# Linear attention rewritten from four batches of eight heads to a pipeline of eight units of four heads

## The reference, cut to what matters

```python
H, DK, DV = (8, 128, 32)
GATE_NORM = 16.0
q = (x @ Wq).reshape(B, T, H, DK) * DK ** -0.5     # x is the layer norm of the input
k = (x @ Wk).reshape(B, T, H, DK)
v = (x @ Wv).reshape(B, T, H, DV)
gk = log_sigmoid(x @ Wgk0 @ Wgk1 + bgk1) / GATE_NORM
# per head: S_t = S_{t-1} * exp(gk_t)[:, None] + k_t^T v_t ;  o_t = q_t @ S_t
g = (x @ Wg).reshape(B, T, H, DV)
o = o * rsqrt(mean(o * o, axis=-1) + EPS)
o = o * g_norm_w * (g * sigmoid(g))
return o.reshape(B, T, H * DV) @ Wo
```

## Time and profile before

| | us |
|---|---|
| median of 3 runs | 1894.39 (1889.34 to 1896.7) |
| the profiled execution, its own time | 1890.36 |
| its span, first to last instruction | 1888.6 |
| linear attention in it, from the first row addition to the last addition to x | 319.77 to 728.97 |
| mean granted TensorE clock | 0.914 of 2.4 GHz |

### The profile page before, as it was taken

The page is one execution under the profiler, slowest core; times in us unless marked ns, Lnnn a source line. Parts: engine busy times, 40 slices in busy tenths (PEclk is TensorE's granted clock), DMA queues, the critical chain, the costliest instruction groups (busy, mean ns, idle before and its releaser), DMA issues. The chain is left out here.

```text
span 1888.6 us, 27025 instructions
## 1 busy us (share of the span) xinstructions
PE 1568.3 (83%) x7662; PEld 1041.7 (55%) x7662; DVE 1092.2 (58%) x2687; ACT 774.5 (41%) x1866; POOL 719.5 (38%) x831
## 2 busy tenths in 40 slices
PE   6869994866868687878996588789999999998798
PEld 4545663534444445545664466555666666665676
DVE  6832222475757546862222788656766766664688
ACT  5523332527171714533333111146655655553211
POOL 3534444440503001544443666035545545543000
PEclk9979997789898988888998788889999999999899
DMA  7209996110101003207995222000000000000000
GB/s 214 65 19 261 304 299 192 56 56 12 57 11 34 1 1 107 78 1 207 290 300 157 81 78 77 7 1 1 1 1 1 1 1 1 1 1 1 8 17 20
DMA packets 83387, 142.46 MB, mean 75 GB/s; under 512 B 15816, under 2 KB 43312, under 8 KB 83296
## 3 DMA queue, kind: packets, MB, share of 16 engines
q1 hardware_dynamic: 53600, 90.96, 16.4%
q0 software_dynamic: 15360, 37.77, 6.8%
q10 hardware_dynamic: 14336, 12.59, 2.3%
HBM read 122.39 MB, written 18.87 MB: 75 GB/s over the span
## 5 line engine op out<-in xcount | busy, mean ns | idle before, releaser
L2206 POOL TENSOR_TENSOR sb_m_prob<-sb_m_prob,sb_m_rinv 128x512 f32<-128x512 f32 x256 | 258.5, 1040 | 289.2 <-DVE sb_m_rinv L2255 289.2
L2162 ACT ACTIVATE sb_m_prob<-m_ps_s,sb_m_nmax 128x512 f32<-128x512 f32 x256 | 173.6, 683 | 204.4 <-DVE sb_m_nmax L2259 204.3
L2259 DVE TENSOR_REDUCE sb_m_nmax<-m_ps_s 128x2 f32<-128x1024 f32 x128 | 156.4, 1222 | 127.9 <-PE m_ps_s L2057 127.8
L1239 POOL DMA_INDIRECT sb_c_rows<-slot_rows,sb_c_at x192 | 193.5, 1008 | 74.7 <-issue 48.4
L1218 DVE TENSOR_TENSOR sb_e_h<-sb_e_sg,e_ps_gu 96x176 f32<-96x176 f32 x128 | 42.7, 334 | 261.7 <-ACT sb_e_sg L1194 261.7
L1156 PE MATMUL e_ps_gu<-e_wgu,sb_e_xT 128*96 128x352 f32 x512 | 178.4, 471 | 12.1 <-ACT sb_e_xT L1188 11.7
L1131 POOL DMA_INDIRECT sb_e_x<-xn_rows,sb_e_index x128 | 121.3, 948 | 102.9 <-POOL sb_e_index L104 96.4
L2065 PE MATMUL m_ps_p<-sb_ident,sb_m_prob 128*128 128x128 f32 x1024 | 136.4, 274 | 15.8 <-ACT sb_m_pT L2170 11.3
L2065 PEld LDWEIGHTS m_ps_p<-sb_ident,sb_m_prob 128*128 128x128 f32 x1024 | 117.9, 141 | 41.1 <-POOL sb_m_prob L2206 13.8
L1173 PE MATMUL e_ps_y<-e_wdn,sb_e_hT 96*96 96x256 f32 x512 | 132.3, 382 | 0.0
L2056 PE MATMUL m_ps_s<-sb_m_latT_high,sb_m_qa 128*128 128x512 f32 x256 | 126.7, 495 | 1.1 <-ACT sb_m_prob L2162 1.1
(11 more groups left out here) (274 smaller groups left out, 3298.1 us busy)
## 6 DMA issues: line engine op xcount, KB each, us to landing
e_wgu<-wgu SPq DMA_DIRECT2D x128, 352.0 KB, 4.7
e_wdn<-wdn SPq DMA_DIRECT2D x128, 192.0 KB, 4.3
slot_rows<-sb_e_y ACTq DMA_DIRECT2D x128, 96.0 KB, 4.2
xn_rows<-sb_r_xn SPq DMA_DIRECT2D x16, 256.0 KB, 2.2
sb_c_rows<-slot_rows,sb_c_at POOLq DMA_INDIRECT x192, 2.8
sb_x<-x SPq DMA_DIRECT2D x4, 512.0 KB, 5.5
sb_e_x<-xn_rows,sb_e_index POOLq DMA_INDIRECT x128, 4.7
sb_g_zm<-wqT SPq DMA_DIRECT2D x1, 2048.0 KB, 8.9
```

Of the source, the lines that this page charges most:

```text
L1239: pool.indirect_dma_start(rows[u][j][:, :], None, k.slot_rows[:, :], bass.IndirectOffsetOnAxis(ap=at[u][:, j:j + 1], axis=0))\
L2162: act.activation(prob[s % 4][:, hh, :], ps_s[s % 2][:, hh, :], ACT.Exp, bias=nmax[s % 2][:, hh:hh + 1], accum_out=rsum[s % 2][:, hh:hh + 1 ...
L2206: pool.tensor_tensor(part, part, rinv[s % 2][:, hh:hh + 1].to_broadcast([P, T]), ALU.mult)\
L2259: dve.tensor_reduce(nmax[s % 2][:, :], ps_s[s % 2][:, :, :], AX, ALU.max, negate=True).then_inc(nmax_ready, 1)
```

## The change

The work is cut into eight units of four heads: unit u is the lower or upper half of the heads of batch u // 2. One function `slot(u)` in each engine's list works on three units: the gates of unit u + 2, the projections, values and output gates of unit u + 1, and the recurrence of unit u. Slots run from -2 to 7. In slots -1, 1 and 3 the next batch is loaded (`loaded_batch`: layer norm, transposes, low-rank product); in slots 2, 4 and 6 a finished batch is projected and added to x (`output_batch`).

The gates are summed without the minimum: ScalarE writes the ReLU of -z in place of z, the running sum adds both inputs in one instruction and runs over all four chunks without a reset, and `edges` takes differences of the sums at middles and ends of chunks (five tiny instructions). One small exponential takes the place of three. The two long exponentials and the subtractions of the middle keep their sizes. The squares, the mean, the normalisation and the output gate are done once for a unit with 512 columns, straight from PSUM, in place of once for a chunk with 256. `xT`, `low`, `mv`, `gw` and the output's PSUM bank have two buffers each; `ps_out` is gone, and the output projection uses the ring. The row additions stand at other places of VectorE's list (tiles 4 to 7 in slot -2, then two tiles in each of slots -1 to 2), and GpSimd issues two tiles' gathers in each of its rounds.

The core of the diff (the bodies of the projections, copies and multiplies change only in their indices):

```diff
+            def gate_parts(u):
+                for h in range(HG):
+                    hh = u % 2 * HG + h
+                    src = use(act, "z", u, h)
+                    act.activation(za[:, u % 2, h, :], src[:, :], ACT.Abs, bias=k.bgk1[:, hh:hh + 1]).then_inc(abs_ready, 1)
+                    act.activation(zm[:, u % 2, h, :], src[:, :], ACT.Relu, scale=-1.0, bias=minus_b[:, hh:hh + 1])\
+                       .then_inc(freed("z", u, h), 1)
...
-                s.after(s.mark(dve.scalar_tensor_tensor(out=zm[:, hs, :], in0=zm[:, hs, :], scalar=0.0, in1=za[:, hs, :],
-                                                        op0=ALU.min, op1=ALU.subtract)))
-                for h in range(half * HG, (half + 1) * HG):
-                    n = s.mark(dve.tensor_tensor_scan(zm[:, h, :], k.chunk_keep[:, :], zm[:, h, :], 0.0, ALU.mult, ALU.add))
...
+            def gate_sums(u, heads):
...
+                    dve.tensor_tensor_scan(part, part, za[:, u % 2, h, :], 0.0, ALU.add, ALU.add).then_inc(sum_ready, 1)
...
+            def edges(u):
...
+                s.mark(dve.tensor_copy(mid[:, :, :], sums[:, :, :, MID]))
+                s.after(s.mark(dve.tensor_copy(ends[:, :, 1:], sums[:, :, :, SUB - 1])))
+                dve.tensor_tensor(spans[:, 0, :, :], mid[:, :, :], ends[:, :, 0:NSUB], ALU.subtract)
+                dve.tensor_tensor(spans[:, 1, :, :], ends[:, :, 1:], ends[:, :, 0:NSUB], ALU.subtract)
+                dve.tensor_tensor(spans[:, 2, :, :], ends[:, :, 1:], mid[:, :, :], ALU.subtract).then_inc(edge_ready, 1)
+                for h in range(HG):
+                    ins = dve.tensor_tensor(za[:, u % 2, h, :].rearrange("p (c s) -> p c s", s=SUB),
+                                            zm[:, u % 2, h, :].rearrange("p (c s) -> p c s", s=SUB),
                                             over(mid[:, h, :], SUB), ALU.subtract)
                 ins.then_inc(cen_ready, 1)
```

TensorE's slot, in which `r` holds for slots 0 to 7 and calls for units outside 0 to 7 do nothing:

```diff
+            def slot(u):
+                r, b_in, b_out = 0 <= u < U, loaded_batch(u), output_batch(u)
+                if r: scores(u, 0)
+                gate(u + 2, 0); projected(u + 1, 0)
+                gate(u + 2, 1); projected(u + 1, 1)
+                gate(u + 2, 2); gate(u + 2, 3)
+                if u >= 1: mean_squares(u - 1)
+                if r: keys_turned(u, 0)
+                projected(u + 1, 2)
+                if r: tiled(u, 0); turned_back(u, 0); scores(u, 1); keys_turned(u, 1)
+                projected(u + 1, 3); values(u + 1)
+                if r: tiled(u, 1)
+                projected(u + 1, 4)
+                if r: turned_back(u, 1)
+                output(b_out, 0); output(b_out, 1)
+                if r: scores(u, 2); keys_turned(u, 2)
+                output_gates(u + 1); projected(u + 1, 5)
+                if r: tiled(u, 2)
+                if b_in is not None: transposes(b_in)
+                projected(u + 1, 6)
+                if r: turned_back(u, 2)
+                output(b_out, 2); output(b_out, 3)
+                if r: scores(u, 3)
+                projected(u + 1, 7)
+                if r: tiled(u, 3)
+                if b_in is not None: low_rank(b_in)
```

ScalarE's and VectorE's slots (here with several calls on a line, as above):

```diff
+            def slot(u):     # ScalarE; zs: u + 2 < U, qs: 0 <= u + 1 < U
+                if b_in is not None: deviations(b_in)
+                if zs: gate_parts(u + 2)
+                if u >= 1: inverse_rms(u - 1)
+                if r: kT_copy(u, 0); kvT_copy(u, 0)
+                if zs: exps(u + 2)
+                if r: kT_copy(u, 1)
+                if zs: lns(u + 2)
+                if qs: value_copy(u + 1)
+                if r: kvT_copy(u, 1); kT_copy(u, 2)
+                if qs: gate_copies(u + 1)
+                if r: kvT_copy(u, 2)
+                if b_in is not None: xT_copies(b_in)
+                if qs: sigmoids(u + 1)
+                if zs: decays(u + 2)
+                if b_in is not None: low_copy(b_in)
+                if r: squares(u)
...
+            def slot(u):     # VectorE
+                n = 2 * u + 10
+                if u == -2: add_rows(4, range(TOPK)); statistics(4); add_rows(5, range(TOPK)); statistics(5)
+                if r: masked(u, 0)
+                scale(u + 1, 0); scale(u + 1, 1); scale(u + 1, 2)
+                if b_in is not None: normalise(b_in)
+                if r: kept = state_added(u, 0, kept)
+                add_rows(n, range(4))
+                if r: masked(u, 1); kept = state_used(u, 1, kept)
+                gate_sums(u + 2, range(1)); scale(u + 1, 3)
+                if u >= 1: normed(u - 1)
+                gate_sums(u + 2, range(1, 2)); scale(u + 1, 4)
+                if r: kept = state_added(u, 1, kept)
+                add_rows(n, range(4, 6)); statistics(n)
+                if r: masked(u, 2); kept = state_used(u, 2, kept)
+                add_out(b_out, 0); add_out(b_out, 1)
+                gate_sums(u + 2, range(2, 3)); scale(u + 1, 5); gate_sums(u + 2, range(3, 4))
+                edges(u + 2); scale(u + 1, 6)
+                if r: kept = state_added(u, 2, kept)
+                add_rows(n + 1, range(3))
+                add_out(b_out, 2); add_out(b_out, 3)
+                if r: masked(u, 3); kept = state_used(u, 3, kept)
+                scale(u + 1, 7)
+                add_rows(n + 1, range(3, 6)); statistics(n + 1)
+                if b_in is not None: low_parts(b_in)
```

More of the change, by code:

```diff
@@ L1288, in linear_attention @@
     a_free = [k.sem(f"g_bank_free{a}") for a in range(A)]
[L1290 to L1311, removed]
+    use_of = {}
     with ExitStack() as ctx:
@@ L1405, in low_rank @@
                     emptied(pe, "tr", b, j)
-                to = take("low", b, 0)
+                to = take("low", b)
                 for c in range(DC):
[L1408 to L1414, removed]
-                for h in heads:
-                    to = take("z", b, h)
-                    given(pe.matmul(to[:, :], wgk1[:, h * DK:(h + 1) * DK], low[:, :], start=True, stop=True), "z", b, h)
@@ L1419, in values @@
[L1419 to L1431 removed]
+                    ins = pe.matmul(to[:, :], k.wgk0[:, c, :], xT[b % 2][:, c, :], start=(c == 0), stop=(c == DC - 1))
@@ new lines, in low_rank, with gate, values @@
+                given(ins, "low", b)
+            def gate(u, h):
+                if u >= U:
+                    return
+                hh = u % 2 * HG + h
+                pe.wait_ge(low_split, batch_of(u) + 1)
+                to = take("z", u, h)
+                given(pe.matmul(to[:, :], wgk1[:, hh * DK:(hh + 1) * DK], low[batch_of(u) % 2][:, :], start=True, stop=True),
+                      "z", u, h)
+            def values(u):
+                if u >= U:
+                    return
+                to, x = take("v", u), xT[batch_of(u) % 2]
+                for j in range(TB):
@@ new lines, in projected @@
+            def projected(u, i):
+                if not 0 <= u < U:
+                    return
+                name, weights = ("q", k.wq0) if i < HG else ("k", k.wk0)
+                hh = u % 2 * HG + i % HG
+                to, x = take("qk", u, i), xT[batch_of(u) % 2]
+                for c in range(DC):
+                    ins = pe.matmul(to[:, :], weights[:, c, hh * DK:(hh + 1) * DK], x[:, c, :],
+                                    start=(c == 0), stop=(c == DC - 1))
+                given(ins, "qk", u, i)
@@ L1595, in z_copies @@
[L1595 to L1604 removed]
+                src = use(act, "low", b)
@@ L1757, in _, with gather @@
+            def gather(n):
+                if n < NT:
+                    gather_tile(pool, k, 0, n, n % 2, rows, at)
             pool.sem_inc(k.sem("c_rows_used"), 2)
@@ new lines, in state_added @@
+            def state_added(u, j, kept):
+                dve.wait_ge(edge_ready, 2 * u + 2)
+                dve.wait_ge(kv_ready, u * (TB - 1) + j + 1)
+                to = kv_dec if j else state
+                dve.tensor_tensor(to[:, :, :], ps_kv[:, :, :], over(edge[u % 3][:, 2, :, j], DV),
+                                  ALU.mult).then_inc(kv_used, 1)
+                dve.wait_ge(kv_used, u * (TB - 1) + j + 1)
+                if j:
+                    s.after(kept)
+                    return s.mark(dve.tensor_tensor(state[:, :, :], state[:, :, :], kv_dec[:, :, :], ALU.add))
+                return s.n
```

799 lines of the change are left out of this document (396 added, 403 removed).

## The result

The changed kernel takes 1845.18 us (median of 4 runs, 1841.6 to 1849.4); the kernel before took 1895.55 beside it (4 runs, 1889.34 to 1897.02). The ratio is 0.9741, with a 95% interval of 0.971 to 0.9772. The prediction was 1845.

A forecast was written before the change was run, and what follows sets the result against it. No engine filled the stretch; engines waited for each other in turn. First scores at 410.5 plus slots 0 to 7 gave 683.5 against 729.0, 45.5 us less; from 1890.4 that gives 1845, own range 1828 to 1862, wider 1816 to 1876.

The forecast's parts named there:

- First scores at 410.5: Lead-in: tile 7 done at 382.3, only then ScalarE touches unit 1's gates; TensorE idle 20 us; before, scores at 417.8.
- (a): Each slot: q head 2 needs a bank freed by ScalarE's z head 3 copy; ready at 9.5, VectorE idles 4 us.
- (b): After q head 2, VectorE works without rest, reaching `edges` 25 us into the slot and leaving it at 28.2.
- (c): Scaling 6, state, mask 3, scaling 7 come only behind `edges`; the next scores wait for scaling 7: slot 5 31 us.
- (d): Even slots: output gate's bank waits for an addition to x; TensorE stalls 1.6 us, VectorE 2.3; slot 4 36.5.
- (e): Row additions on VectorE lengthen the early slots: slot 0 34 + 1, slot 1 39, slot 2 41 us.
- (f): Slot 6 has no gates and follows TensorE: 32 us.
- (g): Slot 7, the bare recurrence, takes 16 us, then normalisation steps 5 and four outputs with additions 4: 25 us.
- The port: GpSimd's gate multiplication locks VectorE out of shared SBUF ports: 1 us added to each slot, up to 9.6 possible.
- The pipeline did not close up: Rival, 12%: the holes of (a) and (d) fill, slots take TensorE's 30.5 us; 80 us less, 1810.
- lockstep: Rival, 18%: each late handover between engines is passed on, slots take 40 us; 13.5 us less, 1877.
- slow clock: Rival, 5%: short holes keep TensorE at 1.2 GHz, slots 59 us, total 2010; half the time low, 44 and 1905.

The follow-up runs named there:

- e3: Changed kernel with ScalarE's four gate copies of a slot ahead of its two small layer-norm instructions (`deviations`): 1846.2 us, one run.
- e6: Changed kernel with `edges` behind scaling 7 in VectorE's list, not ahead of scaling 6: 1883.64 us, one run, ratio 0.984 to before.
- e7: Changed kernel with `edges` behind scaling 6 and the state's addition, ahead of mask 3: 1862.93 us, one run, ratio 0.973 to before.
- e4: Changed kernel with the first two additions to x of even slots ahead of mask 2: 1839.52 us, one run; again 1849.97, ratio 0.966 to before.
- e2: Changed kernel with one VectorE instruction of the old minimum's size ahead of each unit's sums: 1871.19 us, ratio 0.985 to before.
- c1: Changed kernel with the edits of e4 and e5 together: 1858.13 us, ratio 0.969 to before.
- e1: Kernel before with only the new gate arithmetic (ReLU, sums without minimum), all lists in the old order: 1873.19 us, ratio 0.989 to before.
- e5: Changed kernel with TensorE's projection of q head 2 between gate heads 2 and 3: 1854.75 us, one run, ratio 0.969 to before.
- c2: c1 with two gate copies of unit 1 ahead of unit 0's long exponentials in slot -2: 1852.30 us, ratio 0.967 to before.
- c0: The changed kernel repeated without edits on another chip: 1850.15 us, ratio 0.965 to before.

## Why the prediction was right, step by step

**What bounded the kernel before: right.** The recurrence with its turns of waiting is gone from slots 0 to 6, and with it the waits on additions to x.

**First scores at 410.5: 411.3.** The way there was not quite mine. VectorE ended the low part at 355.1, not 352.4: its product began 1 us later than before, and TensorE ran it at half clock (3.75 us for 1.96). Tile 7 was done at 383.9, not 382.3. The hole of 20 us was 22.5. My "only then can ScalarE" named one of two causes that ended together (e3).

**(a) right in place and size.** q head 2 is scaled 10.6 us into slot 4 after a wait of 4.03 (I said 9.5, and 4). The timeline of slot 4 of the changed kernel, from there to the next scores:

```profile
570.86 0.69 DVE L1842 SCALAR_TENSOR_TENSOR sb_g_qp<-g_bank,sb_g_zm 128x512 f32<-128x512 f32 x1 [4.03 <-PE g_bank L1438]
...
575.63 1.23 DVE L1810 TENSOR_TENSOR_SCAN sb_g_zm<-sb_g_zm,sb_g_za 128x512 f32<-128x512 f32 x1 [1.58 <-ACT sb_g_za L1634]
...
577.50 1.98 PE L1438 MATMUL g_bank<-sb_g_xT,sb_wk 128*128 128x512 f32 x4
...
583.38 0.75 DVE L1885 TENSOR_TENSOR sb_x<-g_bank,sb_x 128x256 f32<-128x256 f32 x2
583.85 1.99 PE L1428 MATMUL g_bank<-sb_g_xT,sb_wvg 128*128 128x512 f32 x4 [1.21 <-DVE sb_x L1885]
...
587.66 0.69 DVE L1842 SCALAR_TENSOR_TENSOR sb_g_kp<-g_bank,sb_g_za 128x512 f32<-128x512 f32 x1 [2.40 <-PE g_bank L1438]
...
589.60 1.31 POOL L1750 TENSOR_TENSOR sb_g_gw<-sb_g_g,sb_g_sig 128x512 f32<-128x512 f32 x1 [34.23 <-ACT sb_g_sig L1662]
...
589.81 1.13 DVE L1822 TENSOR_TENSOR sb_g_spans<-sb_g_mid,sb_g_ends 128x16 f32<-128x16 f32 x1
...
591.03 2.48 DVE L1826 TENSOR_TENSOR sb_g_za<-sb_g_zm,sb_g_mid 128x512 f32<-128x512 f32 x4
...
596.27 0.69 DVE L1842 SCALAR_TENSOR_TENSOR sb_g_kp<-g_bank,sb_g_za 128x512 f32<-128x512 f32 x1 [0.16 <-PE g_bank L1438]
...
597.01 1.16 PE L1451 MATMUL g_ps_at<-sb_g_qp,sb_g_kp 128*128 128x128 f32 x8 [0.21 <-DVE sb_g_kp L1842]
```

**(b) nearly.** "Without rest" is wrong: VectorE waits 1.58 us at the first sum for the softplus's logarithm, in slot 5 too. There it leaves `edges` 29.3 us into the slot; I said 28.2, and slot 5 took 32.2 us for my 31. **(c) right**: the last rows have the next scores 0.21 us behind scaling 7; e6 and e7 show that the edges can't simply be moved out of its way.

**(d) right**, in slot 4: 1.21 us of TensorE (I said 1.6), then 2.40 of VectorE for scaling 5 (2.3), and e4 takes the first away. **(e) right in sum, wrong in split**: slots 0 to 2 took 37.8, 38.1, 38.3 for my 35, 39, 41, together 114.2 and 115. **(f)** Slot 6 took 33.7 for 32, with TensorE busy 95% of it. TensorE's work was put too low: 29.5 us a slot against 31.8 busy on average in slots 0 to 6, part of it at the lower clock. **(g)** Slot 7 to the last addition took 25.4 for 25. Slots 3 and 4 took 34.7 and 36.7 for 33.5 and 36.5.

**The port: right.** Above, a difference of 16 elements takes 1.13 us where it falls into GpSimd's multiplication of 1.31; its like beside it takes 0.16. In each of slots 0, 2, 4 and 5 one such small instruction is caught. In slots -1, 1 and 3 the multiplication falls into the subtractions, and four of them take 3.56 to 3.58 us in place of 2.48:

```profile
552.36 3.56 DVE L1826 TENSOR_TENSOR sb_g_za<-sb_g_zm,sb_g_mid 128x512 f32<-128x512 f32 x4
...
553.75 1.63 POOL L1750 TENSOR_TENSOR sb_g_gw<-sb_g_g,sb_g_sig 128x512 f32<-128x512 f32 x1 [35.46 <-ACT sb_g_sig L1662]
```

Over these seven slots this is some 7 us of VectorE, the 1 us a slot that I took. In slots 6 and 7 nothing is lost.

**The sum.** 0.8 late at the first scores, 3.5 over the seven slots (251.5 for 248), 0.4 at the end: the last addition at 688.2 and not 683.5, so linear attention gave 41 us and not 45.5. The rest of the kernel, 5.5 us shorter in this execution by chance, made this up to within a microsecond. The exact agreement is luck, and in a second way too: the prediction put the median of the runs 4 us above its 1845, and it is 1845.18, since the medians differ by 50.4 us and the two traces by 46. The forecast of the stage was 5 us too good by the traces, inside its own range.

**The rivals.** The pipeline did not close up: the holes of (a) and (d) are there, and no edit on (a) filled one without opening another. No lockstep: slots of 32 to 38 us, not 40. No slow clock: 0.95 and more in slots 1 to 6 and 0.89 in slot 0, though e2 and c1 show what a slightly larger hole brings. No table load inside the stage, so ReLU needs none beside the absolute value, exponential and logarithm; as the Trainium skill (ScalarE: Activation LUTs, on table sets) has it.

**How the two halves go together** stays open. In the traces the cheaper sums alone give 13.9 us (e1), the new order that still pays for the minimum 409.6 - 396.1 = 13.5 (e2), and both 41.4, so that 14 would belong to neither alone. The timed runs don't bear that out: 1.1% alone, 1.5% alone, 2.6% together, or 25.2, 27.2 and 50.4 us by the medians; the halves simply add up, with intervals of some 12 us either way on each half, so 14 us could hide in them. One reason for the difference may be which executions were traced: of the kernel before a short one, of e2 the longest of its four. How much of that lies in the stage is not known: from scores to end alone, where two traces of the changed kernel agree to 1.0 us, 10.9 of the 34.3 us belong to neither half. What the traces do show is a mechanism by which work on VectorE can cost more than its own time in the new order, the hole of 2.4 us and the clock behind it; the clock fell so in three of six slots of e2.

## What to carry to other kernels

When an order is rewritten and arithmetic saved at once, time each half alone as well: here either gives 1 to 1.5% and both give 2.6%. One trace of each had 14 us that belonged to neither half, the timed runs had none; before such a remainder is explained it needs more traces and runs than were made here. In the new order work put back on VectorE opened holes of 2.4 us in TensorE's stream, and such a hole can cost its clock. A wait that moves to the next instruction when one operation is advanced has its cause further back; follow it to the engine that was busy all along before reordering. Here the trace points at ScalarE, with logarithm, exponential and copy; no run moved these, so that part is not shown. And where a wait has a named releaser, look for what else ends within a microsecond of it: removing one of two was worth nothing here (e3).

## What the runs showed of the hardware that I had not expected

- Short holes can cost TensorE's clock in a stream that is otherwise dense, but not each time. In e2 six holes of 2.36 to 2.90 us ahead of scaling 3's bank were followed by the level of 1.2 GHz in three slots and by full clock in three. In c1 the hole of 1.83 us was followed by it in three of five, in e5 in one and in c2 in two of five. In slots 2 to 6 of the changed kernel seven holes of 1.19 to 1.55 us were all followed by full clock. The changed kernel has three longer ones, of 4.19, 2.98 and 2.52 us, at the ends of slots 0, 1 and 5, and the lower level came behind each; in its repeat the 2.98 us were followed by full clock. What decides between two equal holes I did not find. The third of them, with the scores at half clock behind it:

```profile
628.35 0.48 PE L1481 MATMUL g_ps_o<-sb_g_qp,sb_g_state_mid 128*32 128x128 f32 x8 [2.52 <-DVE sb_g_state_mid L1855]
...
629.18 2.08 PE L1451 MATMUL g_ps_at<-sb_g_qp,sb_g_kp 128*128 128x128 f32 x8
```

- What falls into GpSimd's multiplication of gate and sigmoid is held up, however small: a VectorE instruction of 0.17 us became 1.13 to 1.18 us long in four slots; in three others the subtractions were held up by 1.1 us.
- A sum with two live inputs takes as long as one with a constant: 1216 ns and, before, 1205 ns for 512 elements.
- On the other chips the traces, all of the changed kernel and its versions, have gaps of 1 to 8 us in which an engine waits for nothing that the profile shows. In the repeat of the changed kernel, in the lead-in:

```profile
348.27 1.47 DVE L1790 TENSOR_SCALAR sb_g_xn<-sb_x,sb_g_mv,sb_g_rstd 128x256 f32<-128x256 f32 x4 [4.00 <-issue]
```

  In the traces of the two kernels and of e1 to e4 VectorE and ScalarE have none in the stage. In c1 the same gap is 7.7 us long, 3.7 of the 5.4 us that it loses ahead of the low part. The kernel before was 21 us slower on the chip of c0 to c2 (1916.61 against 1895.55), the changed one 5 (1850.15 against 1845.18), which is why the ratio there is 0.965 and not 0.974. What makes the gaps, and whether the kernel before has them too, stays open: no run here was made for it, and the kernel before has no trace there.
